# Expert 1's radix search moved behind expert 0's list, in a one-core cross-attention and expert-choice FFN kernel

## The reference

```
x = x + softmax(LN(x) Wq (ctx Wk)^T / 16) (ctx Wv)        # cross attention, per batch
xt = LN(x); S = sigmoid(xt @ Wg).T                        # 8 experts x 4096 scores
G, I = top_k(S, 1024)                                     # each expert picks 1024 rows
hid = gelu(xt[I] @ W1 + b1)                               # 256 -> 1024
out = (hid @ W2 + b2) * G                                 # 1024 -> 256
x = x + scatter_add(out, I)
```

## Time and profile before

| | us |
|---|---|
| median of 3 runs | 512.37 (511.79 to 513.39) |
| profiled execution, its own time | 513.52 |
| its span | 511.8 |
| TensorE matmul busy | 479.5 (94% of the span) |
| VectorE busy | 333.8 (65%) |
| ScalarE busy | 316.2 (62%) |
| mean granted TensorE clock, share of full | 0.966 |

### The profile page before, as it was taken

One profiled execution on the slowest core, in us unless ns is written; L12 is line 12 of the kernel. 1 busy time (PEld: TensorE's weight loads), 2 busy tenths in 40 slices (PEclk: granted clock), 3 DMA queues, 4 the chain that ended last, 5 costly groups with the idle time before them and its releaser, 6 DMA issues.

```text
span 511.8 us, 10692 instructions
## 1 busy us (share of the span) xinstructions
PE 479.5 (94%) x3794; PEld 345.2 (67%) x3794; DVE 333.8 (65%) x763; ACT 316.2 (62%) x605; POOL 286.2 (56%) x392
## 2 busy tenths in 40 slices
PE   7899999999357999999999999999999999999995
PEld 6688888878234558648747845864874784685484
DVE  6788999978884888675385465547538546535721
ACT  3777778866781881594396188359439618826920
POOL 1758999996324067456626726745662671674044
PEclk9999999999556999999999999999999999999999
DMA  6730776566906668447717817844761781673024
GB/s 211 240 118 3 219 193 165 131 185 180 256 13 112 190 148 113 95 135 132 139 37 194 170 20 187 174 51 135 141 130 48 194 157 22 197 95 42 2 32 52
DMA packets 94122, 64.73 MB, mean 126 GB/s; under 512 B 55236, under 2 KB 89992, under 8 KB 94088
## 3 DMA queue, kind: packets, MB, share of 16 engines
q1 hardware_dynamic: 81168, 46.94, 34.9%
q0 software_dynamic: 12288, 17.05, 20.3%
q10 hardware_dynamic: 632, 0.31, 0.2%
HBM read 35.83 MB, written 16.91 MB: 103 GB/s over the span
## 4 chain that ended last, share of the span: by engine, by line
PE 85%; issue 4%; DMA 2%; DVE 2%; ACT 2%; SPq 1%; POOL 1%; POOLq 0%; DVEq 0%; ACTq 0%
PE bank L1245 79%; PE bank L1252 3%; PE bank L1265 1%; DMA ctx<-in_ctx 1%; DMA exT<-ex 1%; SPq L314 1%; PE bank L1550 1%; ACT g L691 1%; POOL xrow L426 1%; DVE oneh L1112 0%; DVE junk L1004 0%; ACT xres L695 0%; PE bank L1348 0%; POOL xrow L424 0%; POOLq L77 0%
## 5 line engine op out<-in xcount | busy, mean ns | idle before, releaser
L1245 PE MATMUL bank<-w2h,xres 128*128 128x256 f16 x1024 | 169.4, 273 | 0.0
L1245 PE MATMUL bank<-exT,w1h 128*128 128x512 f16 (+1 forms) x528 | 155.3, 377 | 3.2 <-DMA exT<-ex 3.2
L1245 PE MATMUL bank<-w2l,xres 128*128 128x256 f16 x512 | 139.6, 273 | 0.0
L523 POOL DMA_INDIRECT out<-yo,ids_s x64 | 100.7, 1574 | 50.2 <-ACT yo L711 27.6
L1169 DVE TENSOR_TENSOR xres<-g,xres 128x512 f16<-128x512 f32 x128 | 87.7, 690 | 52.9 <-ACT xres L695 43.0
L1245 PEld LDWEIGHTS bank<-w2h,xres 128*128 128x128 f16 x1024 | 99.9, 98 | 12.3
L711 ACT ACTIVATE yo<-yt,ge 128x256 f32<-128x256 f32 x63 | 32.0, 508 | 118.8 <-DVE yt L1197 95.2
L691 ACT ACTIVATE g<-bank,b1e 128x512 f32<-128x512 f32 x128 | 88.3, 690 | 25.9 <-DVE b1e L1152 13.5
L1245 PE MATMUL bank<-exT,w1l 128*128 128x512 f16 (+1 forms) x264 | 99.5, 377 | 0.0
L1245 PEld LDWEIGHTS bank<-exT,w1h 128*128 128x128 f16 x528 | 51.7, 99 | 59.1 <-issue 3.3
L695 ACT ACTIVATE xres<-bank,b1e 128x512 f16<-128x512 f32 x128 | 87.7, 685 | 0.0
(11 more groups left out here) (245 smaller groups left out, 769.8 us busy)
## 6 DMA issues: line engine op xcount, KB each, us to landing
w2r<-in_L_ffn_W SPq DMA_DIRECT2D x8, 1024.0 KB
w1r<-in_L_ffn_W SPq DMA_DIRECT2D x8, 1024.0 KB
xres<-in_x SPq DMA_DIRECT2D x8, 512.0 KB, 5.7
out<-xres SPq DMA_DIRECT2D x4, 1024.0 KB, 7.2
ctx<-in_ctx SPq DMA_DIRECT2D x7, 512.0 KB, 4.8
rows_d<-xrow SPq DMA_DIRECT2D x7, 512.0 KB, 3.5
b_bc<-in_L_ffn_b SPq DMA_DIRECT2D x8, 128.0 KB, 3.6
ex<-rows_d,ids POOLq DMA_INDIRECT x64, 3.5
```

The costliest lines, as they stand in the source:

```text
L523: pool.indirect_dma_start(out=rows_out, out_offset=bass.IndirectOffsetOnAxis(ap=ids_s[:, t:t + 1], axis=0), in_=yo[:, t, :], in_offset=Non ...
L1245: last = pe.matmul(out, lhs(a, c), rhs(b, c), start=i == 0, stop=i == len(terms) - 1)
```

## The change

Expert 1's search no longer runs in the gaps of expert 0's. All its ten rounds stand behind expert 0's list. Rounds 1 to 6 follow `first_list`, with dummy matmuls between; rounds 7, 8 and 9 have their folds between the first halves of the early units, and `ranks(1)` behind the last of them. The bias copy of expert 0 goes ahead of the rounds. List 1 is multiplied before units 6 and 7 and read behind unit 7.

```diff
-    Q1 = 4
-    KEEP = 5
+    KEEP, KEEP0 = 5, 7
 ...
-                folded = A_[:, 1] if e and r < Q1 else B_[:, 0]
+                folded = B_[:, 0]                       # in digit and in fold
 ...
                     dve.tensor_scalar(klo01[:], kint01[:, 1], 1.0 / (1 << LO1_BITS), None, ALU.mult).then_inc(s["k01_s"], 1)
-                elif r == 1:
-                    compare(1, 0)
-                elif r == 3:
-                    digit(1, 0)
-                elif r % 2 == 0:
-                    compare(1, r // 2 - 1)
-                else:
-                    digit(1, r // 2 - 1)
 ...
-            compare(1, Q1)
+            compare(1, 0)
 ...
-                b1_of(e, first)
+                if not first:
+                    b1_of(e, first)
 ...
-                    if next1 and u == (KEEP if first else 3):
+                    if next1 and u == (KEEP0 if first else 3):
                         read_list(e + 1)
-                    if u == KEEP:
+                    if u == (KEEP0 if first else KEEP):
                         keep(e, first)
 ...
-            digit(1, Q1)
+            digit(1, 0)
             first_list()
-            relative(1)
-            for r in range(Q1 + 1, R1):
+            b1_of(0, True)
+            for r in range(1, R1):
                 compare(1, r)
                 digit(1, r)
+                if r == HI1 - 1:
+                    relative(1)
             selected(1)
 ...
             for r in range(R1):
                 fold(0, r)
-                if r == 1:
-                    fold(1, 0)
-                if r >= 4 and r % 2 == 0:
-                    fold(1, r // 2 - 1)
                 if r in (3, 5, 7, 9):
                     slow_count((r - 3) // 2)
             ranks(0)
-            fold(1, Q1)
+            fold(1, 0)
             slow_count(4)
 ...
-                    if first and u in (EARLY, EARLY + 1):
-                        list_part(1, 2 * (u - EARLY))
-                        list_part(1, 2 * (u - EARLY) + 1)
+                    if first and u in (EARLY + 2, EARLY + 3):
+                        list_part(1, 2 * (u - EARLY - 2))
+                        list_part(1, 2 * (u - EARLY - 2) + 1)
 ...
-            awake(4)
-            fold(1, 5)
+            for r in range(1, 6):
+                awake(4)
+                fold(1, r)
+                if r == 2:
+                    slow_count(6)
             awake(4)
             fold(1, 6)
-            slow_count(6)
-            awake(4)
-            fold(1, 7)
-            awake(4)
-            fold(1, 8)
-            awake(4)
-            fold(1, 9)
-            awake(6)
 ...
             early_unit(0, 0)
+            fold(1, 7)
             early_unit(1, 0)
+            fold(1, 8)
+            early_unit(3, 0)
+            fold(1, 9)
             ranks(1)
-            for f in range(2, EARLY):
-                early_unit(f, 0)
+            early_unit(2, 0)
```

More of the change, by code:

```diff
@@ L1473, in fold @@
             def fold(e, r):
-                folded = A_[:, 1] if e and r < Q1 else B_[:, 0]
+                folded = B_[:, 0]
                 pe.wait_ge(s[f"cmp_{e}"], r + 1)
```

## The result

The changed kernel took 515.75 us (median of six runs, 513.5 to 516.18) against 511.96 us for the kernel before on the same chip: ratio 1.006, 95% interval 1.0035 to 1.0086, so 2.0 us above the forecast and above its range. The profiled execution took 515.74 us, with a span of 514.0 (before: 513.52 and 511.8). One run of all that follow, 578.34 us at a granted clock of 0.83 where the others have 0.95 or more, was slow and is left out of every comparison.

A forecast was written before the change was run, and what follows sets the result against it. TensorE's stream bounds the kernel from 190 us; before, VectorE's loop sets tile 0. Search gains 0.31, but VectorE's loop starts 1.32 later, leaving +1.3 at tile 0: 512.37 + 1.3 = 513.7 us, range 513.2 to 514.4 (wider 512.0 to 515.0).

The forecast's parts named there:

- The search and the list: Expert 0's search ends 0.52 us earlier without fillers; list, gather and transposes gain 0.31, ends 0.07 and 0.52.
- Round 1's 0.24: Expert 0's search, round 1: reduction was 0.24 us late behind a filler; gained, unless POOL's instructions take it again.
- The first early matmul: TensorE's first early matmul, after expert 0's transposes: comes at 160.07 instead of 160.38, 0.31 us earlier.
- The folds between the units: Expert 1's folds 7 to 9 between early units: 1.46 us apart, fold 9 at 164.25, places at 166.21, 2.87 later.
- The 1.96 from last fold to places: Expert 1, behind fold 9: nothing covers the 1.96 us to the first place instruction, a distance taken from expert 0.
- nothing in the sum depends on what it was slow in: The sum: +1.3 us carries over from the profiled execution, 1.15 slower than the median, to the median, giving 513.7.
- The term that counts: VectorE's first subtraction at 170.33, 1.32 us later; 1.3 remains at tile 0's count, 188.44 becoming 189.7.
- then no wait: TensorE behind tile 0's count, near 189.7: no further wait, so the 1.3 us shift passes unchanged to the end.
- the later list covered: Expert 1's list, read about 181 instead of 177.44: transposes land before 207, in time for its first unit; no cost.
- Rival 1: Early units: clock holds at 1.2 GHz, so TensorE is last at tile 0; +2.2 us, 514.5; chance 0.25.
- Rival 2: Early units: clock stays up with shorter idle time, places at 165.4, loop at 169.5; +0.5 us, 512.9; chance 0.12.
- Rival 3: VectorE's loop to tile 0's count takes 17.7 us without waits, absorbing the delay; -0.4 us, 512.0; chance 0.18.

The follow-up runs named there:

- set 2: Four kernels beside the kernel before; its profile cited here is that kernel unchanged, run again: 510.2 us beside 511.0, ratio 0.9996.
- sets 3 and 4: Two sets that each ran the kernel after unchanged beside the kernel before: 512.11 us, 1.0018 in set 3; 511.85 us, 1.0025 in set 4.
- the first runs: The original measurement of the changed kernel against the kernel before, ahead of the four sets: 515.75 us against 511.96, ratio 1.006.
- set 1: Kernel after unchanged (515.68 us, 1.0074) and three variants: code shifted 1.0074, list put back 1.0046, last early unit ahead of ranks with folds in another bank 1.0073.
- set 3: Kernel after unchanged (512.11 us, 1.0018), later list alone on before (1.0001), after with folds ahead of units (1.0008), after with TensorE's stop filled (1.0014).
- ranks first: Kernel before with expert 1's ranks ahead of the first two early units: 509.83 us, 0.9979 in set 2; 508.72 us, 0.9972 in set 4.
- folds first: Kernel after, expert 1's folds 7 to 9 ahead of early units, ranks behind first unit: list put back 510.97 us, 1.0004; later list kept 511.42 us, 1.0008.
- set 4: Before unchanged (511.74 us, 1.0014), after unchanged (511.85, 1.0025), after with list put back (511.48, 1.0023), before with ranks moved ahead of units (508.72, 0.9972).

## Why the prediction was wrong

**The search and the list: right.** All of the changed kernel's profile is 0.29 earlier when the search begins (the gate's first instruction at 127.04, before at 127.33). Net of that the last fold gains 0.37 for 0.52 and the list 0.24 for 0.31; ScalarE's slow search held the list's second half for 1.03 us, as foreseen. Round 1's 0.24 is there in full: its reduction now waits for the fold, at 130.39 for 130.92, and 0.53 less 0.29 is 0.24. VectorE, rounds 1 and 2 in the kernel after:

```profile
130.39 0.22 DVE L944 TENSOR_REDUCE cnt<-bank 128x7 f32<-128x56 f32 x1 [0.46 <-PE bank L1472]
...
130.86 0.93 DVE L935 SCALAR_TENSOR_TENSOR cmp<-khi,gain,apart 128x224 bf16<-128x224 f32 x1
```

The comparison beside POOL's row splits still takes 0.93 us, 0.88 in the earlier trace rows. The rule of the Trainium skill that VectorE with two SBUF inputs and a reading GpSimd instruction exclude each other (SBUF — State Buffer, "SBUF: two separate sides") agrees with both. The gain fell 0.15 short, inside the 0.24 that the prediction allowed for; these two rows show 0.05 of it, and no run shows the rest.

**The first early matmul: wrong by 2.0, and made good by luck.** Forecast 160.07, measured 158.03, and 157.2 to 158.4 in all profiles of the kernel after and its variants that keep the units' place. The kernel before and its variants go from 158.0 to 160.4. The landing of the transposes is not the fixed distance behind the list that I took from one profile. It brought fold 9 to 162.20 instead of 164.25, 2.05 earlier than forecast, and fold 9's late signal took 1.31 of that back (3.27 from fold to places instead of 1.96). Two errors of opposite sign nearly met, so that the places and the first subtraction came close to the forecast.

**The folds between the units: right in spacing, wrong in what they were compared with.** 1.46 apart forecast, 1.47 measured. Places forecast at 166.21, 2.87 later; measured 165.47, and 163.57 without the late signal. The 1.96 from last fold to places held (163.57 - 161.79 = 1.78). The comparison point was the error: 163.34 is a profile in which the first units ran at half clock, so the prediction's "nothing in the sum depends on what it was slow in" does not hold. Before has its places at 160.38, 162.19 and 163.34 in three profiles, the kernel after at 162.97 and 163.57 in the undisturbed two.

**The term that counts, 1.3 at tile 0: half of it in that pair of profiles, about right on average.** The count moved by 0.63 there (189.07 for the forecast 189.7), or by 0.92 if the head start of 0.29 is taken out. The row at 188.44 names no engine that ended its wait; the same row of set 2 names VectorE (185.51), as the prediction read it. In sets 3 and 4 the ratios are 1.0018 and 1.0025, 0.9 and 1.3 us; the forecast, 513.7 / 512.37, is 1.0026. The runs of the kernel after are the closer together (standard deviation 0.60 and 0.35 us, before 1.26 and 1.05), because its tile 0 hangs on VectorE's rounds and no longer on how fast two units run. Against a fast execution of before it loses (count 186.58 and 187.18 to 185.51), against one with a fallen clock it is level or gains (187.31).

**The step that failed: "then no wait".** The prediction had the stream lost nothing behind the count of tile 0, and called the later list covered. The list is covered in sets 2 to 4. In the first runs and set 1 it puts tile 1 where a late signal of 2.1 us falls, and the count of tile 2 waits for it. Put back in that same set, it gave 1.6 us of 3.7. Of the other 2.1, the term above accounts for 0.9 to 1.3, what the kernel after costs in the sets without late signals. What is left is about the size of fold 9's late signal, 1.06 at the count of tile 0 between the profiles with and without it; no run takes that signal away by itself, so this part is argued and not shown.

**The rivals.** Rival 1, the clock coming too late, had a true observation, the half clock until 169.2, but filling the stop moved the time by 0.16 and the count of tile 0 still waited for VectorE. Rival 2, a clock that stays up, is what the profile of set 3 shows up to fold 9 (1.0 from 152.7 to 162.9, places at 162.97), but the kernel before gains at least as much from it (count 185.51 for 188.44). Rival 3, the loop absorbing all, is out: from the first subtraction to the count of tile 0 VectorE takes 19.49 us in three profiles of the kernel after, 19.43 before, and not 17.7, and the count still waits 0.80 to 0.91.

**What stays open.** What holds TensorE's signals, and why in some sets alone. A shift of the code left tile 1's late, another bank left fold 9's; one chip number had sets with and without. Taking the transposes or the gathers away was not tried, nor a run without the records, and neither ranks first nor folds first was run in a set with late signals.

## What to carry to other kernels

A wait in one profile is a sample: before a difference of 1 us is forecast from landmarks, ask which of them move with the clock or a DMA landing, and compare like with like. Subtract ratios only within one set; across two, 0.7 us looked like 2.1. And a step that only waits for data already there (here expert 1's ranks) belongs ahead of a wait for a transfer, not behind it: one moved line gave 0.9972 and 0.9979.

## What the runs showed of the hardware

TensorE can have run a matmul and those behind it at full pace while its signal reaches VectorE 0.4 to 2.2 us later than usual: 2.40 us instead of 0.31 in tile 1. It happened in all six profiles of the first runs and set 1, always while POOL's DMA queue moved packets (at fold 9 without the transposes), and in none of twelve later ones with the same transfers. The six traces also lack over a fifth of the records of semaphore updates.

TensorE's granted clock was 1.00 through a stop of 2.24 us (162.6 to 164.8) and fell to 0.50 only 1.0 us after the engine had started again, from 165.8 to 169.2, in the early units. The same kernel had no such fall in two other profiles, with stops of 2.54 us (set 1) and 0.85 us (set 4). The fall cost nothing that the ratios show (1.0018 with it, 1.0025 without), since VectorE's loop and not TensorE sets tile 0.
